# A two-layer transformer and state space program on one core: gating, one norm's moments and the last rows handed to other engines

## The reference

```python
x = x + L0_attn(_layernorm(x))      # 16 heads of 64, softmax
x = x + L0_ffn(_layernorm(x))       # 8 experts, the best one per row
x = x + L1_attn(_layernorm(x))      # state space mixer, below
x = x + L1_ffn(_layernorm(x))       # 8 experts, all summed, one gate per row
# L1_attn, per batch:
h = x @ fc1_w.T + fc1_b
xc, z = jnp.split(h @ in_proj_w.T, 2, axis=-1)
u = silu(conv4(xc) + conv_b)
dt_low, Bm, Cm = jnp.split(u @ x_proj_w.T, [8, 24], axis=-1)
dt = softplus(dt_low @ dt_proj_w.T + dt_proj_b);  A = -exp(A_log)
hstate = exp(dt * A) * hstate + (dt * u) * Bm     # 16 states for each of 256 channels, over 1024 steps
y = (hstate * Cm).sum(states) + u * D
y = y * silu(z)
out = (y @ out_proj_w.T) @ fc2_w.T + fc2_b
```

## Time and profile before

| | us |
|---|---|
| median of 3 runs | 1200.11 |
| the runs | 1197.57, 1200.11, 2362.79 |
| profiled execution, its own time | 1205.08 |
| span of its trace | 1203.8 |
| outside the span | 1.28 |
| granted TensorE clock, mean | 0.984 |

### The profile page before, as it was taken

The page is one execution under the profiler, slowest core; times in us unless marked ns, Lnnn a source line. Parts: engine busy times, 40 slices in busy tenths (PEclk is TensorE's granted clock), DMA queues, the critical chain, the costliest instruction groups (busy, mean ns, idle before and its releaser), DMA issues.

```text
span 1203.8 us, 19482 instructions
## 1 busy us (share of the span) xinstructions
...
## 2 busy tenths in 40 slices
...
DMA packets 38060, 68.85 MB, mean 57 GB/s; under 512 B 5936, under 2 KB 24112, under 8 KB 37968
## 3 DMA queue, kind: packets, MB, share of 16 engines
...
q0 software_dynamic: 1024, 2.10, 0.5%
q10 hardware_dynamic: 1984, 0.98, 0.3%
...
## 4 chain that ended last, share of the span: by engine, by line
PE 78%; issue 6%; POOL 6%; DVE 5%; ACT 3%; DMA 1%; another core or an unknown queue 1%; POOLq 0%; SPq 0%; DVEq 0%; ACTq 0%
PE psum L583 19%; PE psum L552 16%; PE psum L569 6%; PE psum L599 5%; PE psum L556 5%; POOL hc L1997 4%; PE psum L952 3%; PE psum L661 3%; PE psum L861 3%; PE psum L935 3%; PE psum L614 2%; PE psum L634 2%; PE psum L727 2%; PE psum L738 2%; PE psum L793 1%
## 5 line engine op out<-in xcount | busy, mean ns | idle before, releaser
L1910 POOL TENSOR_TENSOR psums<-psums,prob 128x1024 f32<-128x1024 f32 x180 | 426.7, 2371 | 106.6 <-ACT prob L1024 84.0
L1414 DVE TENSOR_REDUCE mx<-psum 128x2 f32<-128x1024 f32 x256 | 301.9, 1219 | 214.5 <-PE psum L569 211.9
L1024 ACT ACTIVATE prob<-psum 128x1024 f32<-128x1024 f32 x256 | 243.1, 1025 | 218.2 <-PE psum L556 218.2
L583 PE MATMUL psum<-prob,V 128*64 128x512 f32 x1024 | 258.4, 604 | 0.0
L1997 POOL TENSOR_TENSOR hc<-hs,cc 128x1024 f32<-128x1024 f32 x64 | 151.5, 2367 | 32.7 <-DVE hs L1710 30.8
L1710 DVE TENSOR_TENSOR_SCAN hs<-dA,psum 128x1024 f32<-128x1024 f32 x64 | 146.3, 2286 | 2.1
L861 PE MATMUL psum<-hc,ident 128*128 128x512 f32 x256 | 124.5, 609 | 5.4 <-POOL hc L1997 3.0
L583 PEld LDWEIGHTS psum<-prob,V 128*64 128x64 f32 x1024 | 62.0, 136 | 98.4 <-issue 92.7
L1910 POOL TENSOR_TENSOR psums<-prob 128x1024 f32<-128x1024 f32 x30 | 71.4, 2380 | 63.5 <-ACT prob L1024 63.5
L552 PE MATMUL psum<-q_hi,k_hi 64*128 64x512 f32 x512 | 108.5, 419 | 0.0
L556 PE MATMUL psum<-guard,row_one 64*128 64x512 f32 x512 | 101.7, 393 | 2.2 <-DMA guard<-mrow 2.2
...
## 6 DMA issues: line engine op xcount, KB each, us to landing
...
```

The source lines that it names most:

```text
L583: ins = pe.matmul(A.O[HALF[s], :], A.V[pair % 2][:, j, s * DH:(s + 1) * DH], A.prob[unit(pair, c, j) % NPB][:, s * CH:(s + 1) * CH], start ...
L1024: act.activation(A.prob[n % NPB][:, :], slots.bank("score", pair, c, j).rearrange("p s n -> p (s n)"), ACT.Exp, scale=float(DH) ** -0.5).t ...
L1414: dve.tensor_reduce(K.A.mx[:, :, t, c], slots.bank("max", pair, t, c), AXX, ALU.max).then_inc(*slots.inc("max", pair, t, c))
L1910: pool.tensor_tensor(total[:, :], (K.A.prob[(n - 1) % NPB] if j == 1 else total)[:, :], K.A.prob[n % NPB][:, :], ALU.add).then_inc(*K.psum ...
```

## The change

It does four things.

1. The outputs of three of the four halves leave DVE. ACT copies Y from PSUM to the SBUF tile `du` (`act_leave`), at steps 17, 33 and 49; POOL multiplies that with silu(z) in SBUF (`pool_gated`), at steps 18, 34 and in dense step 4. The fourth stays on DVE. `outp` waits for `Y_gated`.
2. The moments of norm 5 leave DVE. ACT sums the rows of four tiles with the accumulator output of an Identity (`act_means`), POOL negates the means (`pool_centre`), ACT sums the squares with Square and the negated mean as bias (`act_squares`). This is done twice, at steps 8 to 10 and wholly in step 11. The root is `pool_root_of_sums`, at step 12.
3. What follows the moments is moved a unit sooner: `lnrows` to step 13, the transposes to 14, their copies and fc1 to 15, the mixes to 16 to 23, `xpj` to 25, `dtp` to 26, softexp to 27. The second half of z of the first batch (`inp_out 0 3`) moves from step 13 to 14, du of the second half from 12 to 13, fc2bias from 20 to 31, `du 1 0` stays at 29 and `dt 1 0` goes to 28.
4. The last chunk is finished in two halves: two activations, two times two transposes (the second pair in a free bank), two times two additions, two stores.

Left out of the diff: the entries of new steps and semaphores in their tables, one more store to wait for at the end, the dropped special case of norm 5 in `dve_moments`.

```diff
--- before.py
+++ after.py
@@ -61,8 +61,10 @@
 PRE_EW = 11
-
-ACT_ROWS, XDR_UNIT = (1, 2, 5, 6), 26
+LAST_ROWS, LAST_BANK = (B - 1, SEQ // CH - 1), B * (SEQ // CH) * M1 - 1
+
+
+ACT_ROWS, XDR_UNIT = (1, 2, 5, 6), 25
 LAST = PAIRS - 1
...
@@ -318,13 +320,13 @@
         beside[t] += [("back", 1, t)]
         beside[t + 2] += [("rescale", t)]
     one = {0: [("expo", 1), ("softexp", 0, 1), ("softlog", 0, 1), ("first_skip",)], 1: [("rate", 1)], 5: [("e1_load",)], 6: [("wturn",)],
-           7: [("wscale",), ("readd", 0)], 8: [("inp", 0, 2)], 9: [("inp_out", 0, 2), ("dt", 0, 1)], 10: [("wback", 0), ("wback", 1), ("readd", 1)],
-           11: [("wback_out", 0), ("wback_out", 1)], 12: [("inp", 0, 3), ("du", 0, 1)], 13: [("inp_out", 0, 3), ("lnhalf", 5), ("lnroot", 5)], 14: [("lnrows", 5)], 15: turned(5), 16: [("fc1", 1), ("fc1_out", 1)],
-           17: [("mix", 0, 0)], 18: [("mix", 0, 1)], 19: [("mix", 0, 2)], 20: [("mix", 0, 3), ("fc2bias", 0)],
-           21: [("silu", 1, 0), ("mix", 1, 0)], 22: [("mix", 1, 1)], 23: [("mix", 1, 2)], 24: [("mix", 1, 3)],
-           25: [("silu", 1, 1)], XDR_UNIT: [("xpj", 1), ("xpj_out", 1), ("xdr", 1)],
-           27: [("dtp", 1, 0), ("dtp_out", 1, 0)], 28: [("softexp", 1, 0)], 29: [("softlog", 1, 0), ("dt", 1, 0), ("du", 1, 0)],
-           35: [("outp", 0, 0)], 36: [("outp_out", 0, 0), ("outp", 0, 1)], 37: [("outp_out", 0, 1), ("fc2", 0, 0)],
+           7: [("wscale",), ("readd", 0)], 8: [("inp", 0, 2), ("means", 0)], 9: [("inp_out", 0, 2), ("dt", 0, 1), ("centre", 0)], 10: [("wback", 0), ("wback", 1), ("readd", 1), ("squares", 0)],
+           11: [("wback_out", 0), ("wback_out", 1), ("means", 1), ("centre", 1), ("squares", 1)], 12: [("inp", 0, 3), ("lnroot", 5)], 13: [("lnrows", 5), ("du", 0, 1)], 14: [("inp_out", 0, 3)] + turned(5)[:2], 15: turned(5)[2:] + [("fc1", 1), ("fc1_out", 1)],
+           16: [("mix", 0, 0)], 17: [("leave", 0, 0), ("mix", 0, 1)], 18: [("gated", 0, 0), ("mix", 0, 2)], 19: [("mix", 0, 3)],
+           20: [("silu", 1, 0), ("mix", 1, 0)], 21: [("mix", 1, 1)], 22: [("mix", 1, 2)], 23: [("mix", 1, 3)],
+           24: [("silu", 1, 1)], XDR_UNIT: [("xpj", 1), ("xpj_out", 1), ("xdr", 1)],
+           26: [("dtp", 1, 0), ("dtp_out", 1, 0)], 27: [("softexp", 1, 0)], 28: [("softlog", 1, 0), ("dt", 1, 0)], 29: [("du", 1, 0)],
+           31: [("fc2bias", 0)], 33: [("leave", 0, 1)], 34: [("gated", 0, 1)], 35: [("outp", 0, 0)], 36: [("outp_out", 0, 0), ("outp", 0, 1)], 37: [("outp_out", 0, 1), ("fc2", 0, 0)],
            38: [("fc2", 0, 1), ("fc2_out", 0, 0)], 39: [("fc2_out", 0, 1)], 40: [("lnvar", 6), ("lnroot", 6), ("dtp", 1, 1)],
            41: [("dtp_out", 1, 1), ("lnrows", 6)], 43: turned(6)[:2] + [("softexp", 1, 1), ("softlog", 1, 1), ("fc2bias", 1)],
            44: turned(6)[2:] + [("dt", 1, 1), ("inp", 1, 2)], 45: [("inp_out", 1, 2), ("du", 1, 1)], 46: [("inp", 1, 3)],
...
@@ -332,6 +334,7 @@
     for e in range(E1):
         one[48 + e - 1] = one.get(48 + e - 1, []) + [("w1hi", e), ("w1lo", e)] * (e > 0)
         one[56 + e] = [("w2hi", e), ("w2lo", e)]
+    one[49] = [("leave", 1, 0)] + one[49]
     for i in range(EARLY_UPS):
         one[49 + i] += [("up1", i)]
         one[50 + i] += [("pre", i)]
...
@@ -352,7 +355,7 @@
 def dense_order():
-    ahead = {4: [("output", 1, 1)], 7: [("outp_out", 1, 0)], 8: [("outp_out", 1, 1)], 9: [("fc2_out", 1, 0)], 10: [("fc2_out", 1, 1)],
+    ahead = {4: [("gated", 1, 0), ("output", 1, 1)], 7: [("outp_out", 1, 0)], 8: [("outp_out", 1, 1)], 9: [("fc2_out", 1, 0)], 10: [("fc2_out", 1, 1)],
              11: [("lnvar", 7), ("lnroot", 7)], 12: [("e1_lg", 0), ("e1_root", 0)], 13: [("lnrows", 7)], 15: [("e1_norm", 0)],
              17: [("e1_exp", 0)], 18: turned(7)[2:], 19: [("e1_top", 0)], 21: [("xhi", 1, 0)], 22: [("xhi", 1, 1)],
              23: [("xlo", 1, 0), ("e1_lg", 1), ("e1_root", 1)], 24: [("xlo", 1, 1)], 25: [("e1_norm", 1)], 31: [("e1_exp", 1)], 33: [("e1_top", 1)]}
...
@@ -886,7 +889,9 @@
 def pe_outp(K, pe, b, c):
     X, work = K.X, K.work
-    pe.wait_ge(X.Y_taken, KI * (b + 1))
+    pe.wait_ge(X.Y_gated, KI if b == 0 else KI * B - 1)
+    if b:
+        pe.wait_ge(X.Y_taken, KI * B)
     if b == 0 and c == 0:
         pe.wait_ge(*K.ld["outp"])
     if work.free("outp", b, c):
...
@@ -956,8 +961,27 @@
         ins.then_inc(*work.full.inc("sum1", b, c))
+def pe_last_turn(K, pe):
+
+    Y, work = K.Y, K.work
+    yT = Y.yT[(B * NC - 1) % 2]
+    pe.wait_ge(Y.half_summed, 1)
+    pe.wait_ge(*work.free("turn1", *LAST_ROWS))
+    for t in range(2):
+        ins = pe.transpose(work.bank("turn1", *LAST_ROWS)[:, t * P:(t + 1) * P], yT[:, t * P:(t + 1) * P], K.ident[:, :])
+    ins.then_inc(Y.half_turned, 1)
+    pe.wait_ge(*work.empty("sum1", *LAST_ROWS))
+    pe.wait_ge(*work.empty("up1", LAST_BANK))
+    for t in range(2, 4):
+        ins = pe.transpose(work.bank("up1", LAST_BANK)[:, t * P:(t + 1) * P], yT[:, t * P:(t + 1) * P], K.ident[:, :])
+    ins.then_inc(*work.full.inc("turn1", *LAST_ROWS))
+
+
 def pe_turn1(K, pe, b, c):
     Y, work = K.Y, K.work
+    if (b, c) == LAST_ROWS:
+        pe_last_turn(K, pe)
+        return
     pe.wait_ge(*work.empty("sum1", b, c))
     pe.wait_ge(*work.free("turn1", b, c))
     for t in range(4):
...
@@ -1043,6 +1067,22 @@
                              bias=K.shift[:, t:t + 1])
         if t % 4 == 3:
             ins.then_inc(*K.act_rows.inc(n, t // 4))
+
+
+def act_means(K, act, g):
+
+    act.wait_ge(K.returned, NT + 4 * (g + 1))
+    for t in range(4 * g, 4 * g + 4):
+        ins = act.activation(K.xrows[:, NT + t, :], K.x[:, NT + t, :], ACT.Identity, scale=1.0 / D, accum_out=K.mv[:, t, 0:1])
+    ins.then_inc(K.X.means_done, 1)
+
+
+def act_squares(K, act, g):
+
+    act.wait_ge(K.X.centred, g + 1)
+    for t in range(4 * g, 4 * g + 4):
+        ins = act.activation(K.xrows[:, NT + t, :], K.x[:, NT + t, :], ACT.Square, bias=K.shift[:, t:t + 1], accum_out=K.mv[:, t, 1:2])
+    ins.then_inc(K.X.squares_done, 1)
 def act_rescale(K, act, t):
...
@@ -1224,6 +1264,13 @@
         act_decay(K, act, u + 2)
+def act_leave(K, act, b, k):
+
+    act.wait_ge(K.X.added, (b * KI + k + 1) * NS)
+    act.wait_ge(K.X.gain_done, (b * KI + k + 1) * NS)
+    act.copy(K.X.du[b][:, k, :], K.X.Y).then_inc(K.X.Y_taken, 1)
+
+
 def act_outp(K, act, b, c):
     X, work = K.X, K.work
     act.wait_ge(*work.full.at("outp", b, c))
...
@@ -1244,7 +1291,7 @@
     if e == 0:
         act.wait_ge(*K.ld["e1_w1"])
-        act.wait_ge(K.X.Y_taken, KI)
+        act.wait_ge(K.X.Y_gated, KI)
         act.wait_ge(K.X.xdr_done, B)
         act.wait_ge(K.X.C_stored, 16 * B)
     act.copy(K.Y.w1s[0][:, e, :], K.Y.ew1[:, e, :]).then_inc(K.Y.w_hi, 1)
...
@@ -1301,6 +1348,12 @@
         act.wait_ge(Y.b2_done, 1)
     if i >= 2:
         act.wait_ge(*K.work.full.at("turn1", *divmod(i - 2, NC)))
+    if (b, c) == LAST_ROWS:
+        act.activation(Y.yT[i % 2][:, 0:2 * P], K.work.bank("sum1", b, c)[:, 0:2 * P], ACT.Identity, bias=Y.b2s[:, 0:1]).then_inc(
+            Y.half_summed, 1)
+        act.activation(Y.yT[i % 2][:, 2 * P:CH], K.work.bank("sum1", b, c)[:, 2 * P:CH], ACT.Identity, bias=Y.b2s[:, 0:1]).then_inc(
+            *K.work.inc("sum1", b, c))
+        return
     act.activation(Y.yT[i % 2][:, :], K.work.bank("sum1", b, c), ACT.Identity, bias=Y.b2s[:, 0:1]).then_inc(
         *K.work.inc("sum1", b, c))
...
@@ -1369,10 +1422,7 @@
 def dve_half_moments(K, dve, n):
-    if n == LN_E0 + 1:
-        dve.wait_ge(*K.slots.empty("out", LAST, 0))
-    else:
-        dve.wait_ge(K.returned, NT + NT // 2)
+    dve.wait_ge(*K.slots.empty("out", LAST, 0))
     for t in range(4):
         dve.bn_stats(K.stats[:, t, :], K.x[:, n % 2 * NT + t, :])
...
@@ -1699,10 +1749,6 @@
     if u == 0:
         dve.wait_ge(X.dt_done, 1)
     dve.tensor_tensor(X.gain[u % 2], X.gain[u % 2], (X.du if u else X.dt)[b][:, k, :], ALU.mult).then_inc(X.gain_done, 1)
-    if n == 2 and u > NS:
-        dve_output(K, dve, *divmod(u // NS - 1, KI))
-    if u == 14:
-        dve_moments(K, dve, LN_SSM + 1)
     dve.wait_ge(X.gain_done, u + 1)
     dve.wait_ge(X.decay_done, u + 1)
     if u >= 3:
...
@@ -1810,12 +1856,19 @@
 def dve_added(K, dve, b, c):
     Y = K.Y
-    dve.wait_ge(*K.work.full.at("turn1", b, c))
+    last = (b, c) == LAST_ROWS
+    if last:
+        dve.wait_ge(Y.half_turned, 1)
+    else:
+        dve.wait_ge(*K.work.full.at("turn1", b, c))
     dve.wait_ge(Y.gated, b + 1)
     for t in range(4):
         tt = 4 * c + t
         xs = K.x[:, b * NT + tt, :]
-        ins = dve.scalar_tensor_tensor(out=xs, in0=K.work.bank("turn1", b, c)[:, t * P:(t + 1) * P],
+        if last and t == 2:
+            ins.then_inc(Y.half_added, 1)
+            dve.wait_ge(*K.work.full.at("turn1", b, c))
+        ins = dve.scalar_tensor_tensor(out=xs, in0=(K.work.bank("up1", LAST_BANK) if last and t >= 2 else K.work.bank("turn1", b, c))[:, t * P:(t + 1) * P],
```

(41 more changed lines are left out.)

10 lines of the change are left out of this document (6 added, 4 removed).

## The result

By the runs within 1.5% of the fastest of their kernel (all but one of before, of 2362.79 us, which nothing on record explains) the changed kernel takes 1.0036 times as long as the one before, 95% interval 1.0022 to 1.0050: 4.3 us slower (2.6 to 6.0), median 1202.07 us against 1198.47 in the same comparison. That is within 2% and inside the range given, - 1.3 to + 5.3 us, though the interval reaches past its upper end. The forecast was 2.3 slower.

A forecast was written before the change was run, and what follows sets the result against it. DVE bounds the recurrence up to 928, then PE; + 6.6 - 1.2 - 2.4 + 0.75 - 1.0 - 0.4 = + 2.35 us, so 1207.4 for a profiled execution and 1202.4 median, range 1198.8 to 1205.4.

The forecast's parts named there:

- Passes at 2.1, a wait at scan 14: ACT's four passes for the moments take 2.1 us each; DVE's 2.1 saved at unit 14 go in waiting for ACT.
- The root at 918.7, fc1 at 928.8: Chain to fc1: POOL's root ends at 918.7; rows, decay, silu, decay and copies on ACT let fc1 start at 928.8.
- Gain 17 late by 6.6 with the clock: DVE's gain of unit 17 comes 5.1 us late behind fc1, plus 1.5 for PE's slower clock after idling.
- rival A: fc1 does not hold up PE, so all DVE savings pay: - 8.0 us, 1192.1; chance 0.08 in full, 0.12 for half.
- The lower end of - 1.3: Range's fast end: passes of 1.1, gain 17 3.0 late, no clock loss; the sum is - 1.3 us.
- Nothing made up to 31, output 18 worth nothing: Units 17 to 31: PE sets the pace, the delay stays, and the 1.6 us saved at output 18 vanish.
- - 1.2 at unit 32: Gain 32: its wait for du goes, saving 1.2 us.
- - 2.4 at output 34: Unit 34: the output no longer stands in DVE, saving 2.4 us.
- + 0.75 at units 37 and 38: Units 37 and 38: outp waits for POOL and a second outp lengthens one unit, costing 0.75 us.
- - 1.0 at output 50: Unit 50: the output leaves DVE, saving 1.0 us.
- - 0.4 for the tail: End of the kernel: finishing the last chunk in halves saves 0.4 us, between 0 and 0.9.
- Rival B: ACT's squares: Square needs table loads, three ahead of the root, 3.84 us; sum + 6.2, 1206.3; chance 0.10.

The follow-up runs named there:

- E1: Changed kernel with the silu of z (inp_out 0 3) moved from step 14 to 13, ahead of norm 5's rows; ratio to the kernel before 1.0022.
- E4: Changed kernel with silu at step 13, fc2bias back at step 19 and POOL's last gate at step 52; ratio to the kernel before 0.9981, again 0.9983.
- E5: Kernel before with only the outputs moved, their copy to ACT and product with z to POOL; ratio to the kernel before 1.0001.
- E6: Kernel before with only the moments of norm 5 moved to ACT, root still at step 13; ratio to the kernel before 0.9999.
- E7: Kernel before with only the last chunk finished in two halves; ratio to the kernel before 0.9994.
- E2: Changed kernel with fc2bias back from step 31 to 19; ratio to the kernel before 1.0021; scan 0 to end 340.24 us, second execution 337.58.
- E3: Changed kernel with POOL's last gate (gated 1 0) moved from dense step 4 to recurrence step 52; ratio to the kernel before 1.0007.
- E9: Kernel before with outputs moved to ACT and POOL, last gate at step 52 and tail in halves, moments left on DVE; ratio to it 0.9982.

## Why the prediction was right, and where not

The sum was + 2.35; the traces give + 2.72, the ratio + 4.3. The main mechanism, a chain to fc1 that costs more than DVE saves and is never made up, is right. That the number came so near is luck. The term of gain 17 was 1.9 too large and the tail gave 0.5 more than forecast, while units 37 and 38 cost 1.8 and the last gate 1.1 more: + 0.5 in all. And the median of 1202.07 is close to the 1202.4 forecast because the base, 1200.11 of three runs, was 1.6 above the later median of 1198.47.

- **Passes at 2.1, a wait at scan 14:** wrong. They took 1.17 and 1.54, nearer to the lower bound of 1.1. Decay 14 was in time, so DVE kept the 2.1 us that the forecast had it spend waiting for ACT. I had charged the read of the sum in full, and its row overlaps with its neighbours. The estimate from the Trainium skill's page "ScalarE: Activation LUTs" (section "What ACT_TABLE_LOAD costs"), 0.29 a tile without the read, was for an activation with a per-partition bias. The squares are of that form and take 0.385 with the read; the means have no such bias, and take 0.29 with it.
- **The root at 918.7, fc1 at 928.8:** these are 52.4 and 62.5 behind scan 0. Measured 50.35 and 62.1. That fc1 came so near its place is luck: the chain began 2.0 sooner, and lost that again on two steps that I left out. The transposes waited 3.1 us (911.49 to 914.59) for banks held until the silu (E1), and fc1, though ACT's copies were done at 60.4, stood behind the sum in PE's queue. I had read what each step waits for on its own engine and not who holds the PSUM it writes.
- **Gain 17 late by 6.6 with the clock:** 64.5 against 59.8 before, 4.7 late. I had all of it at unit 17; 3.2 of it fell on unit 16, since the transposes stand in step 14, ahead of spread 16. The spread and the sum at 1.2 GHz (1.20 and 3.02, at 2.4 they take 1.02 and 1.88) put the clock's loss at an estimated 1.3, where I took 1.5, which leaves 3.4 for the chain where I had 5.1. The row right behind the 3.07 us of idle in the earlier trace rows, by which I had the clock fall, is the spread, still at full speed with 0.73; the slow row is the sum after it. So that term was 1.9 too large, and rival A, in full, wrong: even E4, with the silu mended, has scan 17 2.2 late.
- **The lower end of - 1.3:** it does not follow from its own terms. 3.0 - 1.2 - 2.4 + 0.75 - 1.0 - 0.4 is - 0.25, and - 0.75 with the tail at 0.9.
- **Nothing made up to 31, output 18 worth nothing:** right (+4.75 at scan 17, +4.77 at 31; E5 shows it alone).
- **- 1.2 at unit 32:** right, -1.25.
- **- 2.4 at output 34:** right against this trace, by luck: the wait of 1.26 in the earlier trace rows belonged to that execution. In the two others with this order, E6 and E7, the unit takes 4.56 and 4.50 and the output's going is worth 1.05 to 1.1. With that the trace of after would be 4.1 over before, where the ratio has 4.3 (2.6 to 6.0). I do not rest more on it: other ratios and traces here differ by up to 2.5 us, which stays unexplained.
- **+ 0.75 at units 37 and 38:** wrong, + 2.5 (E2). "The fc2 additions, norm 6 and fc2bias stay as they are" is the step that failed: the diff moves fc2's bias from 20 to 31, 2.36 us on the engine for which outp waits. With the bias back and PE at 2.4 GHz it is + 1.0 (E2's second execution, and E5).
- **- 1.0 at output 50:** right, -1.0.
- **The last gate, in dense step 4:** the sum has no term for it, and it costs 1.1 (E3): beside it DVE's splits are slower.
- **- 0.4 for the tail:** -0.9, the upper bound (E7).

Of the signs named, these came: no load near the squares, a granted clock below 0.9, units of 3.9 up to 25, units 34 and 50 at 3.45. DVE's idle time before scan 14 did not; before gain 17 it was 1.44 us, not 3 to 6, since gain 16 had waited first, and before gain 37 1.95, not 0.3. None of the signs of being wrong came. Rival B fell with the first decay behind the squares: no load. E4 and E9 are 0.2% faster than before.
